# One Trainium2 core, a graph network layer pair: the second gather pass with slots spread by DMA, one 192-column matmul a tile, attributes row by row, finished rows turned by eight transposes

## The reference

```python
src = edge_index[0]
dst = edge_index[1]
x = jnp.concatenate([h[src], h[dst], edge_attr], axis=-1)
x = _bn_relu(x @ Wm1 + bm1, gm1, betm1)
```

## Time and profile before

| what | value |
|---|---|
| three runs | 19933.13, 19948.8, 19953.17 us, median 19948.8 |
| the profiled execution's own time | 19907.32 us |
| its span | 19904.8 us |
| GpSimd busy over the span | 61% |
| VectorE busy | 38% |
| TensorE busy (weight loads) | 32% (25%) |
| ScalarE busy | 9% |
| mean granted TensorE clock | 0.614 of full speed |

### The profile page before, as it was taken

The page is one execution under the profiler, slowest core; times in us unless marked ns, Lnnn a source line. Parts: engine busy times, 40 slices in busy tenths (PEclk is TensorE's granted clock), DMA queues, the critical chain, the costliest instruction groups (busy, mean ns, idle before and its releaser), DMA issues. The chain is left out here.

```text
span 19904.8 us, 173884 instructions
## 1 busy us (share of the span) xinstructions
PE 6330.2 (32%) x43954; PEld 5014.5 (25%) x44061; DVE 7650.9 (38%) x16776; ACT 1873.1 (9%) x2728; POOL 12116.0 (61%) x12232
## 2 busy tenths in 40 slices
PE   0000000000021211212215744444444444458997
PEld 0000000000010110111105733333333333334885
DVE  5999000000144544544458861111111111226664
ACT  2000000000000000000000001111111111124333
POOL 0388777777677777777756735555555555530442
PEclk6555555555555555555558976666666666668998
DMA  1000000000012222222233311111111111155321
GB/s 49 3 3 2 5 5 5 5 5 5 18 50 52 51 51 53 50 52 50 52 39 98 121 57 40 41 41 40 42 40 41 41 40 42 40 87 189 94 93 54
DMA packets 678218, 917.93 MB, mean 46 GB/s; under 512 B 284316, under 2 KB 431387, under 8 KB 677916
## 3 DMA queue, kind: packets, MB, share of 16 engines
q0 software_dynamic: 322304, 245.26, 8.0%
q1 hardware_dynamic: 294236, 440.78, 7.2%
q10 hardware_dynamic: 61632, 231.44, 3.0%
HBM read 648.03 MB, written 268.67 MB: 46 GB/s over the span
## 5 line engine op out<-in xcount | busy, mean ns | idle before, releaser
L681 POOL DMA_INDIRECT big<-b_d,big x3424 | 3233.4, 944 | 2873.7 <-ACT big L669 1825.9
L602 POOL DMA_INDIRECT rec_d<-big x3224 | 3594.8, 1115 | 1516.1 <-issue 982.7
L839 POOL DMA_INDIRECT big<-h_d,big x3424 | 3763.8, 1099 | 1234.3 <-issue 1007.8
L867 PE MATMUL ps<-big,ones_bc 128*128 128x512 bf16 x750 | 356.4, 622 | 5217.9 <-PEq L140 5016.8
L1359 DVE TENSOR_TENSOR big<-ps,big 128x1024 f32<-128x1024 f32 x214 | 262.0, 1224 | 4450.4 <-PE ps L722 3082.9
L873 PE MATMUL ps<-big 128*128 x3424 | 635.5, 367 | 3504.0 <-PEq L140 1774.0
L722 PE MATMUL ps<-big 128*128 x10272 | 876.5, 213 | 2616.6 <-issue 2615.2
L867 PEld LDWEIGHTS ps<-big,ones_bc 128*128 128x128 bf16 x856 | 93.1, 127 | 5370.6 <-issue 5370.6
L1574 POOL TENSOR_SCALAR big<-iota_f,big 128x128 f32<-128x128 f32 x1070 | 636.6, 613 | 1263.6 <-PE ps L1656 750.0
L873 PEld LDWEIGHTS ps<-big 128*128 128x128 bf16 x3424 | 443.2, 141 | 3806.6 <-issue 3774.2
L722 PEld LDWEIGHTS ps<-big 128*128 128x128 bf16 x10272 | 606.8, 107 | 2838.3 <-issue 2817.5
(11 more groups left out here) (353 smaller groups left out, 11991.8 us busy)
## 6 DMA issues: line engine op xcount, KB each, us to landing
big<-e_d SPq DMA_DIRECT2D x428, 512.0 KB, 4.5
rows_d<-big ACTq DMA_DIRECT2D x214, 544.0 KB
big<-rows_d SPq DMA_DIRECT2D x214, 544.0 KB, 3.4
e_d<-big ACTq DMA_DIRECT2D x214, 512.0 KB
big<-rec_d SPq DMA_DIRECT2D x858, 64.0 KB, 3.3
big<-h_d,big POOLq DMA_INDIRECT x3424
big<-b_d,big POOLq DMA_INDIRECT x3424
rec_d<-big POOLq DMA_INDIRECT x3224
```

Source lines behind the costliest of these rows:

```text
L602: gp.indirect_dma_start(rec_d, bass.IndirectOffsetOnAxis(ix_stage[b][:, j:j + 1], 0), rec_stage[b][:, j * REC:(j + 1) * REC], None).then_i ...
L681: gp.indirect_dma_start(q.G[b][:, t * q.row:(t + 1) * q.row], None, table, bass.IndirectOffsetOnAxis(q.idx[b][:, t:t + 1], 0)).then_inc(q. ...
L839: gp.indirect_dma_start(G[g][:, t * ROW:(t + 1) * ROW], None, h0_d, bass.IndirectOffsetOnAxis(idx[g % 2][:, t:t + 1], 0)).then_inc(gath[g] ...
```

## The change

Only the second gather pass is rewritten (and one DRAM tensor of 1.1 MB added). For a block:
- ACT makes the indices and a bf16 copy of the slots (L1338 and L1339 of the changed kernel), two blocks ahead. Records and gather buffers are four deep.
- SP stores the slots of a block to `slots_d` in the order of edges (L1305, 2048 elements of 2 bytes), waits, and loads that row of 4 KB into all 128 partitions (L1309), then the record of block k+4 (L1312). VectorE compares with the partition's number (L1431), which gives the one-hots with the slot in the partition: nothing is turned or copied.
- TensorE takes all three pieces of a tile in one matmul of 192 columns (L1408), four tiles to a PSUM half of 2 banks. The attributes come row by row: one transpose of the records (L1384), then two float32 matmuls of 512 columns with a block-diagonal weight (L1390). VectorE adds the gathered rows to them (L1449), gives `G` back, and for each four tiles sums the three pieces in PSUM (L1456) and adds (L1459). TensorE turns the finished rows with eight transposes (L1398), in the middle of the next block's selection. ACT copies and stores as before (L1349, L1353).

```diff
+    slots_d = dram("slots_d", (NBLK, TB * P), BF16)
...
-        q1 = Pass("l1", D)
+        QT = TB // 4
+        G = [take(TB * D) for _ in range(4)]
+        rec = [take(TB * REC) for _ in range(4)]
+        rec3 = [r.rearrange("p (t w) -> p t w", w=REC) for r in rec]
+        idx = [take(TB, I32) for _ in range(2)]
+        slot = [take(TB // 2, BF16) for _ in range(4)]
+        SB = [take(TB * P // 2, BF16) for _ in range(2)]
+        OT = [take(TB * P // 2, BF16) for _ in range(2)]
         SUM = [take(TB * D) for _ in range(2)]
         E1 = [take(TB * D) for _ in range(2)]
-        watt = take(TB // 2 * P)
-        recT = take(P)
+        GA = take(TB * D)
+        watt = take(TB * D)
...
+        XSB = [ps[:, h * 1024:(h + 1) * 1024].rearrange("p (b w) -> p b w", w=512) for h in range(2)]
+        XSW = [x[:, :, 0:6 * D] for x in XSB]
+        XSUM = [x[:, :, 6 * D:8 * D].rearrange("p b (t d) -> p b t d", t=2) for x in XSB]
+        XST = [x.rearrange("p b (t w) -> p b t w", w=3 * D) for x in XSW]
+        XSQ = [x.rearrange("p b (t q d) -> p b t d q", t=2, q=3) for x in XSW]
+        AT = ps[:, 2048:2048 + TB * D]
+        RECT = AT[:, 0:P]
+        E1P = ps[:, 3072:3072 + TB * D]
...
+        def every_block(eng, body):
+            for g in range(4):
+                body(g, 0, g, g == 0)
+            with eng.Fori(1, NBLK // 4) as i:
+                for g in range(4):
+                    body(g, i, i * 4 + g)
+            for g in range(NBLK % 4):
+                body(g, NBLK // 4, NBLK - NBLK % 4 + g, False, g == NBLK % 4 - 1, True)
...
+                def spread(g, i, k, first=False, last=False, end=False):
+                    b = g % 2
+                    consume(sp, slot_rdy[b])
+                    sp.dma_start(slots_d[ds(k, 1), :].rearrange("k (t p) -> p (k t)", p=P), slot[g],
+                                 allow_slow_non_contiguous=True).then_inc(slot_st, 16)
+                    consume(sp, slot_st, 16)
+                    consume(sp, sb_free[b])
+                    sp.dma_start(SB[b], slots_d[ds(k, 1), :].to_broadcast([P, TB * P])).then_inc(sb_in[b], 16)
+                    if not end:
+                        consume(sp, rec_free[g], 2)
+                        sp.dma_start(rec[g], rec_blk[ds(k + 4, 1), :, :].rearrange("k p w -> p (k w)")
+                                     ).then_inc(rec_in[g], 16)
...
+                def gather(g, i, k, *_):
+                    consume(gp, idx_rdy[g % 2])
+                    gp.sem_inc(rec_free[g], 1)
+                    consume(gp, g_free[g])
+                    for t in range(TB):
+                        gp.indirect_dma_start(G[g][:, t * D:(t + 1) * D], None, b_d,
+                                              bass.IndirectOffsetOnAxis(idx[g % 2][:, t:t + 1], 0)).then_inc(gath[g], 16)
+                every_block(gp, gather)
...
+                def indices(g):
+                    b = g % 2
+                    consume(a, rec_in[g], 16)
+                    a.sem_inc(rec_seen, 1)
+                    a.activation(idx[b], rec3[g][:, :, 1], ACT.Copy).then_inc(idx_rdy[b], 1)
+                    a.activation(slot[g], rec3[g][:, :, 0], ACT.Copy).then_inc(slot_rdy[b], 1)
+                def turned(b):
+                    consume(a, rt_rdy)
+                    a.activation(recT[b], RECT, ACT.Copy).then_inc(rcp_rdy, 1)
+                def keep(b, k):
+                    consume(a, e_rdy)
+                    consume(a, bn_free[b])
+                    consume(a, e_st[b], 16)
+                    a.activation(E1[b], E1P, ACT.Copy).then_inc(e_cp, 1)
+                    consume(a, e_cp)
+                    a.sem_inc(bn_rdy, 1)
+                    a.sem_inc(e_free, 1)
+                    a.dma_start(e1_d[ds(k, 1), :, :].rearrange("k p w -> p (k w)"), E1[b]).then_inc(e_st[b], 16)
+                def step(g, i, k, first=False, last=False, end=False):
+                    hold(a, "a", gath[g], i * (16 * TB) + 16 * TB)
+                    a.sem_inc(g_rdy[g], 1)
+                    if not end:
+                        indices((g + 2) % 4)
+                    if not last:
+                        turned((g + 1) % 2)
+                    if not first:
+                        keep((g + 1) % 2, k - 1)
...
+                def turn(g):
+                    consume(t, rec_seen)
+                    consume(t, at_free)
+                    t.transpose(RECT, rec[g], ident[:, :]).then_inc(rt_rdy, 1)
+                def attributes(g):
+                    consume(t, rcp_rdy)
+                    t.sem_inc(rec_free[g], 1)
+                    for n in range(2):
+                        m = t.matmul(AT[:, n * 512:(n + 1) * 512], recT[g % 2], watt[:, n * 512:(n + 1) * 512],
+                                     start=True, stop=True)
+                    m.then_inc(at_rdy, 1)
+                def turn_sums(b):
+                    consume(t, sum_rdy)
+                    consume(t, e_free)
+                    for n in range(TB // 2):
+                        m = t.transpose(E1P[:, n * P:(n + 1) * P], SUM[b][:, n * P:(n + 1) * P], ident[:, :])
+                    m.then_inc(e_rdy, 1)
+                def step(g, i, k, first=False, last=False, end=False):
+                    consume(t, ot_rdy)
+                    chunks = chunks_of(t, k * (TB // 2))
+                    for q in range(4):
+                        consume(t, xs_free[q % 2])
+                        for n in range(QT):
+                            o = q * QT + n
+                            m = t.matmul(XST[q % 2][:, n // 2, n % 2, :], OT[g % 2][:, o * P:(o + 1) * P],
+                                         T1[:, ds(chunks[o // 2] * (3 * D), 3 * D)], start=True, stop=True)
+                        m.then_inc(xs_rdy[q % 2], 1)
+                        if q == 1 and not first:
+                            turn_sums((g + 1) % 2)
+                        if q == 2 and not last:
+                            turn((g + 1) % 4)
+                    if not last:
+                        attributes((g + 1) % 4)
...
-                def first_product(b, k):
-                    hold(t, "t", s_sum, k + 1)
-                    hold(t, "t", s_rcp, k + 1)
-                    for p in range(TB // 2):
-                        o = E1P[:, p * P:(p + 1) * P]
-                        t.matmul(o, SUM[b][:, p * P:(p + 1) * P], ident[:, :], start=True, stop=False)
-                        m = t.matmul(o, watt[:, p * P:(p + 1) * P], recT, start=False, stop=True)
-                    m.then_inc(e_done, 1)
-                def step(b, i, k):
-                    hold(t, "t", q1.rec_in[b], i * 16 + 16)
-                    turn_records(b, k)
-                    turn_onehots(t, q1, 1 - b, i + b, k + 1)
-                    first_product(b, k)
-                    src_rows(t, q1, k + 1, T1)
...
+                def onehot(b):
+                    consume(v, sb_in[b], 16)
+                    v.tensor_scalar(OT[b], SB[b], iota_p[:, 0:1], None, ALU.is_equal).then_inc(s_oh, 1)
+                    consume(v, s_oh)
+                    v.sem_inc(ot_rdy, 1)
+                    v.sem_inc(sb_free[b], 1)
...
-                def add_rows(b, i, k):
-                    hold(v, "v", q1.gath[b], i * (16 * TB) + 16 * TB)
-                    hold(v, "v", q1.xs_done, k + 2)
-                    v.tensor_tensor(SUM[b], XSF, q1.G[b], ALU.add).then_inc(s_sum, 1)
-                    hold(v, "v", s_sum, k + 1)
-                    v.sem_inc(q1.g_free[b], 1)
-                    v.sem_inc(q1.xs_free, 1)
...
+                def step(g, i, k, first=False, last=False, end=False):
+                    b = g % 2
+                    if not last:
+                        onehot((g + 1) % 2)
+                    consume(v, g_rdy[g])
+                    consume(v, at_rdy)
+                    v.tensor_tensor(GA, AT, G[g], ALU.add).then_inc(s_e, 1)
+                    consume(v, s_e)
+                    v.sem_inc(g_free[g], 1)
+                    v.sem_inc(at_free, 1)
+                    for q in range(4):
+                        consume(v, xs_rdy[q % 2])
+                        x = XSUM[q % 2]
+                        v.tensor_reduce(x, XSQ[q % 2], AX, ALU.add).then_inc(s_e, 1)
+                        v.wait_ge(s_e, 2 * q + 1)
+                        w = slice(q * QT * D, (q + 1) * QT * D)
+                        v.tensor_tensor(SUM[b][:, w].rearrange("p (b t d) -> p b t d", b=2, t=2), x,
+                                        GA[:, w].rearrange("p (b t d) -> p b t d", b=2, t=2), ALU.add).then_inc(s_e, 1)
+                        v.wait_ge(s_e, 2 * q + 2)
+                        v.sem_inc(xs_free[q % 2], 1)
+                    v.sem_inc(s_e, -8)
+                    v.sem_inc(sum_rdy, 1)
+                    if not first:
+                        statistics((g + 1) % 2, k - 1)```

```

(1 more changed line is left out.)

112 lines of the change are left out of this document (44 added, 68 removed).

## The result

The changed kernel takes 20309.1 us (median of 4 runs, 20294.9 to 20337.5), the kernel before 19942.1 us beside it (4 runs). The ratio is **1.0186, 95% interval 1.0168 to 1.0203**, 367 us more. The forecast was 19040 us, with a range from 18350 to 19700.

The account below looks back on a forecast made before the run. Gathers at 20.0 us a block plus pauses for slow TensorE were to bound the second pass: 23.07 us instead of 27.32. Over 213 blocks that saves 905 us, 19949 - 905 = 19040 us, range 18350 to 19700.

Parts of the forecast that it names:

- Where the pass stood and what bounded it: Second gather pass before the change: 27.32 us a block, 20.0 of gathers and 7.3 waiting for indices because TensorE is late.
- The costs of instructions: New block's work: TensorE 7.7 us and VectorE 12.1 us, both hidden behind 20.0 us of gathers.
- the paragraph on SP and DMA: Slot store, broadcast and record load: SP's chain takes 9 to 10 us, against 20 us of gathers, so no gain or loss.
- The price: Slot store L1305: 2048 2-byte pieces take 2.4 us plus about 2 us to land, priced from a store of 256-byte pieces.
- The threshold: SP's chain would set the pace only if the slot store took over 15 us, 7 ns a piece.
- Two blocks of lead: SP's chain of slot store and broadcast, 9 to 10 us, was set against two blocks of lead.
- D: Rival, slower: TensorE handshakes come late in every block under gathers; 29.2 us a block, 20350 us; chance 0.07.
- F: Rival, slower: slot store pieces go one after the other and set the pace; 45 us a block, 23700 us; chance 0.02.
- C: Rival: TensorE's slowness under gathers eats most of the gain; 25.5 to 27.1 us a block, 19560 to 19900 us; chance 0.15.
- E: Rival: the pass waits for something else the old one had too; 27.3 us a block stays, same time; chance 0.03.
- The trickle: TensorE matmuls slow to 1.4 us each under unbroken gathers, forcing pauses every 3.8 blocks; 22.1 to 23.8 us a block.
- at 1.4 us a matmul, 20 us yield 14: TensorE in the new loop: 14 matmuls under a block's gathers where 27 are needed, a deficit of 13 a block.

Follow-up runs that it names:

- e8: The e4 kernel plus a 2.0 us GpSimd memset between the eighth and ninth gather of each block: 18945.3 us, ratio 0.9583.
- e17: The kernel before plus a 2.0 us GpSimd memset between the eighth and ninth gather of each second-pass block: 19406.9 us, ratio 0.98.
- e18: The e4 kernel plus a 0.95 us GpSimd memset between the eighth and ninth gather of each block: 19091.0 us, ratio 0.9641.
- e15: The changed kernel run again as it is, beside the kernel before: 20481.4 us, ratio 1.0315.
- e6: Changed kernel with slots stored side by side in 128 pieces, plus 2048 2-byte pieces 512 bytes apart into an unread tensor: 19264.4 us, ratio 0.974.
- e3: Changed kernel with half the slots stored as 1024 2-byte pieces, the other half as 128 pieces of 16 bytes: 20148.0 us, ratio 1.0187.
- e5: Changed kernel with one gather a block instead of 16 in the second pass: 20002.5 us, 27.80 us a block.
- e4: Changed kernel with slots taken from records TensorE transposes one block earlier, stored as 16 rows of 256 bytes: 19333.2 us, ratio 0.9735.
- e9: Same change as e17, run where the kernel before took only 18318.9 us: 18845.7 us, ratio 1.0281.

## Why the prediction was wrong

**Where the pass stood and what bounded it** was right for the chip it was read from: GpSimd's pace 20.0 us, the rest a wait for TensorE's late signals. e8, e17 and e18 show by experiment that the lateness depends on breaks.

**The costs of instructions** were right but for L1431. Forecast and measured, in us: L1431 1.2 and 0.78; L1449 1.22 and 1.23; L1456 0.96 and 0.97; L1459 0.42 and 0.43; L1439 0.69 and 0.69; a 512-column f32 matmul 1.1 and 1.02; the gather 0.944 and 0.951; the broadcast 4.5 to landing and 4.1 from issue to the one-hot that waits for it. VectorE's busy time of a block is 8.9 us, just below the 9 to 11 that were named.

**The step that failed is the paragraph on SP and DMA**, in three places.
1. The price: "2048 take 2.4 us plus about 2 us to land" became 16.9 in the median (18.0 in e15). The row it came from had 256-byte pieces, each with memory of its own; these 2-byte pieces have 128 neighbours in the same 256 bytes. e6 shows that the estimate was fair for pieces that stand apart, e3 that the count does not matter. The pieces leave at about the forecast rate; it is their completion that is late. The sign that the prediction named for this, a store of more than 15 us, came.
2. The threshold: "only if the store took over 15 us". The sum took SP's own chain alone. But "both have a block's time to spare" was false: the record load waits for TensorE's attributes, and the next store stands behind it. The rest of the round is 29.3 - 16.5 = 12.8 us, so the store sets the pace from 20.0 - 12.8 = **7.2 us** on, half of what was written (worked out from this round, not tried). It could have been read from the code: the order of three lines in one queue, and who gives back `rec_free`.
3. "Two blocks of lead": the indices have it, the slots do not, since SP takes a block's store up only after the record load of the block before.

**The rivals.** D named 29.2 us a block and 20350 us, 0.1 us and 41 us from the result, and is wrong all the same: in e5 the period stays at 27.8 us with one gather a block, and in the changed kernel's rows VectorE waits for TensorE's groups 0.3 us at a time. Its match is luck. F named the mechanism, the slot store, at 45 us a block and 0.02: its own argument, 2-byte pieces one after the other, is nearer to the truth than the row that spoke against it. (The rule quoted from the Trainium skill, DMA: Bandwidth & Descriptors, section Rules for kernel authors, against a rearranged pattern in a plain DMA, was right in its direction. Its 19 times are against a hardware transpose, and no run here has one; against the turned store's 2.4 us the scattered one's 16.9 are seven times.) The chances written for what was left out of the range (two thirds of C, with D, E and F) also add up to 0.22, more than the two in ten that were claimed.

**The trickle** as the forecast's main term, 22.1 to 23.8 us a block with a pause every 3.8 blocks, could be tested once the store was out of the way, and its mechanism was wrong. The sign that it named, gaps of over 0.7 us between the matmuls of a group, is absent in the changed kernel and in e4; the groups run in 0.8 us and their signals are late. The pause comes in 107 of 213 blocks of e4 and lasts 9.2 us in the mean: 20.0 + 9.2 / 2 gives 24.6, against 24.76 measured. So the size of a pause was right, and it comes every second block instead of every 3.8. The step "at 1.4 us a matmul, 20 us yield 14" counted matmuls; what limits is that VectorE and TensorE take turns, and in the rows of e4 one group of four costs 9 to 10 us. That the kernel without its slow store takes some 19330 us and lies inside the range is therefore in part luck. The trickle of the kernel before is real all the same, and it goes with the chip: from 12500 to 16500 us neighbouring selection matmuls (L725) start up to 2.8 us apart in e17, and at most 0.18 us apart in e9.

**Outside the pass** the change was to cost nothing, within 20 us; it was 57 us, 43 of them in the first pass, whose period differs from run to run (22.6 to 23.3 us a block over all profiles).

## What to carry to other kernels

When a transfer is priced, ask three things: how long its pieces take to send, when its completion is signalled, and how many pieces write into the same few hundred bytes. A transposing store of 4 KB in 2-byte elements cost 16.9 us where one in 16 pieces of 256 bytes cost 2.4. And before calling a chain "hidden", follow it until it closes: in a queue that issues several blocks' transfers in order, a wait for block k's consumer stands ahead of block k+1's producer, and the round to compare with the pace is the whole one.
